# Two attention stages of a decoder kernel: scores and exponents handled by single PSUM bank, the norm a step earlier, the tops' read-back later

## The reference, cut to what matters

```python
x = _layernorm(x + _L0_attn_ref(x, ...))      # norm, q k v, rope, causal softmax, Wo, then a gelu FFN
x = _layernorm(x + _L0_xattn_ref(x, ctx, ...))
x = _layernorm(x + _L0_ffn_ref(x, ...))       # norm, attention over all positions, then a mixture of experts
# inside an attention, per head h:
scores = q[h] @ k[h].T / sqrt(8)              # + causal mask in the first
att[h] = softmax(scores) @ v[h]
```

## Time and profile before

| | |
|---|---|
| median of 3 runs | 2877.28 us (2876.09 to 2885.17) |
| the profiled execution | 2881.1 us, span of the trace 2879.3 us |
| mean granted TensorE clock | 0.860 |
| busy over the span | PE 2162.3 us (75%), PEld 1334.6 (46%), DVE 1974.9 (69%), ACT 1383.5 (48%), POOL 1329.9 (46%) |
| stage `at0`, 56 to 300 us | PE 210.8 of 244 us |
| stage `at1`, 774 to 990 us | PE 148.5 of 216 us |

### The profile page before, as it was taken

One profiled execution on the slowest core, in us unless ns is written; L12 is line 12 of the kernel. 1 busy time (PEld: TensorE's weight loads), 2 busy tenths in 40 slices (PEclk: granted clock), 3 DMA queues, 4 the chain that ended last, 5 costly groups with the idle time before them and its releaser, 6 DMA issues. The chain is left out here.

```text
span 2879.3 us, 48880 instructions
## 1 busy us (share of the span) xinstructions
PE 2162.3 (75%) x19339; PEld 1334.6 (46%) x19339; DVE 1974.9 (69%) x3225; ACT 1383.5 (48%) x2007; POOL 1329.9 (46%) x1015
## 2 busy tenths in 40 slices
PE   3889666776367699999689999999899975553703
PEld 1455444555145566666345554554445543342303
DVE  4565455887455456666358988888988884887576
ACT  1444315554155533333176666666666642221497
POOL 3432244555333100000059889898898892332001
PEclk7899877787578899999789999999999997665856
DMA  4331010000243110000122222222222221000001
GB/s 104 78 89 47 10 32 18 18 16 5 69 99 82 37 55 1 1 1 1 43 67 78 78 76 78 72 85 80 69 78 75 75 67 33 15 15 9 0 0 30
DMA packets 137521, 135.76 MB, mean 47 GB/s; under 512 B 22720, under 2 KB 131024, under 8 KB 134096
## 3 DMA queue, kind: packets, MB, share of 16 engines
q1 hardware_dynamic: 129744, 131.07, 15.8%
q10 hardware_dynamic: 7552, 1.58, 0.3%
HBM read 109.73 MB, written 16.58 MB: 44 GB/s over the span
## 5 line engine op out<-in xcount | busy, mean ns | idle before, releaser
L2293 POOL TENSOR_TENSOR mam_h<-mam_h,mam_c_all 128x1024 f32<-128x1024 f32 x256 | 658.0, 2585 | 91.2 <-DVE mam_h L2365 91.2
L2365 DVE TENSOR_TENSOR_SCAN mam_h<-mam_decay,mam_ps_b 128x1024 f32<-128x1024 f32 x256 | 574.9, 2275 | 101.0 <-PE mam_ps_b L1996 95.3
L1996 PEld LDWEIGHTS mam_ps_b<-mam_diag,mam_duT 64*128 64x128 f32 x4096 | 255.1, 193 | 217.4 <-DVE mam_h L2365 127.0
L2187 ACT ACTIVATE mam_decay<-mam_delta,mam_a_neg 128x508 f32<-128x508 f32 x512 | 331.4, 710 | 32.8 <-DVE mam_h L2365 28.6
L1996 PE MATMUL mam_ps_b<-mam_diag,mam_duT 64*128 64x128 f32 x4096 | 301.1, 290 | 53.8 <-DVE mam_h L2365 42.0
L760 DVE TENSOR_REDUCE at_top<-at_ps_s 128x8 f32<-128x1024 f32 x128 | 156.8, 1225 | 197.8 <-PE at_ps_s L485 196.5
L2015 PE MATMUL mam_ps_y<-mam_h,all_ident 64*64 64x512 f32 x2048 | 255.1, 614 | 13.6 <-POOL mam_h L2293 13.6
L1513 ACT ACTIVATE moe_silu<-moe_ps_g 128x512 f32<-128x512 f32 x144 | 85.9, 597 | 227.3 <-PE moe_ps_g L1456 205.2
L624 ACT ACTIVATE at_e<-at_ps_e 128x1024 f32<-128x1024 f32 x128 | 131.2, 1025 | 116.4 <-PE at_ps_e L485 112.2
L2269 POOL TENSOR_TENSOR mam_diag<-mam_halves,mam_b_col 128x512 f32<-128x512 f32 x128 | 137.6, 1075 | 41.3 <-ACT mam_b_col L2161 41.3
L1468 PEld LDWEIGHTS moe_ps_d<-moe_w_down,moe_hidden 128*128 128x128 f32 x1152 | 139.8, 192 | 33.9 <-issue 33.9
(11 more groups left out here) (357 smaller groups left out, 4503.3 us busy)
## 6 DMA issues: line engine op xcount, KB each, us to landing
mam_c_all<-mam_c_rows SPq DMA_DIRECT2D x256, 256.0 KB, 3.4
at_rows<-at_split SPq DMA_DIRECT2D x64, 192.0 KB, 2.9
at_q<-at_rows SPq DMA_DIRECT2D x32, 192.0 KB
at_k<-at_rows SPq DMA_DIRECT2D x32, 192.0 KB
at_q<-at_rows SPq DMA_DIRECT2D x32, 128.0 KB
at_k<-at_rows SPq DMA_DIRECT2D x32, 128.0 KB
all_x_all<-in_x SPq DMA_DIRECT2D x8, 256.0 KB, 4.8
at_q<-at_rows SPq DMA_DIRECT2D x32, 64.0 KB
```

The lines of the kernel that those rows point to most:

```text
L1996: last = nc.tensor.matmul(ps_b[:, slot, odd, :, at // 2, x:x + HT], duT[r, d, s % DT, at, :], diag[r, chunk % SLOTS, at, :, :], start=True ...
L2187: last = nc.scalar.activation(decay[:, s % SLOTS, :, n, :, 1:T], src, ACT.Exp, scale=a_neg[:, d, s % DT, st:st + 1])
L2293: nc.gpsimd.tensor_tensor(flat(h[:, slot, :, :, :, :]), flat(h[:, slot, :, :, :, :]), flat(c_all[:, chunk, :, :, :, :]), ALU.mult).then_in ...
L2365: nc.vector.tensor_tensor_scan(row(h[:, s % H_SLOTS, :, :, :, :]), row(decay[:, s % SLOTS, :, :, :, :]), row(ps_b[:, s % 2, :, :, :, :]), ...
```

## The change

`both` works one bank at a time: in its first pass the scores' bank 0 (upper rows) with the exponents' bank 1 (lower rows), in its second the scores' bank 1 with the exponents' bank 0. Waits and masks are per bank too. `find_top` becomes two reductions and `exponentiate` two activations, each waiting for its bank and each counted, so the counts that others wait for double. The norm's statistics and root move from step 3 to step 2, and the application from the end of step 0 to the end of the step 3 before it. `read_top(s-2)` moves to the end of ACT's step, behind the second `exponentiate`.

```diff
--- before.py
+++ after.py
@@ -459,56 +459,57 @@
                     return last
                 fill(("v", n), emit)
 
-            def scores_free(b, x):
+            def scores_free(b, x, r):
                 slot, cols = slot_of(b)
-                if x == 0 and b % G == 0:
+                if x == 0 and r == 0 and b % G == 0:
                     for which in range(2):
                         pe.wait_ge(landed[which][slot], LANDED * (b // G // RING + 1))
                 if b > 0 or x > 0:
-                    pe.wait_ge(top_ready, 2 * b + x)
-
-            def exponents_free(b, x):
-                if x == 0:
+                    pe.wait_ge(top_ready, 4 * b + 2 * x + r - 1)
+
+            def exponents_free(b, x, r):
+                if x == 0 and r == 1:
                     pe.wait_ge(top_landed[b % 2], 16 * 2 * (b // 2 + 1))
                 if b > 0 or x > 0:
-                    pe.wait_ge(e_ready, 2 * b + x)
-
-            def masks(b, x, dst, stationary, moving):
+                    pe.wait_ge(e_ready, 4 * b + 2 * x - r)
+
+            def mask(dst, r, stationary, moving):
+                nc.tensor.matmul(dst[:, r, :, :], stationary[:], repeat(moving[:], NJ), start=True, stop=False, skip_group_check=True)
+
+            def product(b, x, r, j, dst, left, right, rows):
+                slot, cols = slot_of(b)
+                at = slice(r * HALF, r * HALF + rows)
+                return nc.tensor.matmul(dst[:, r, j, :], left[at, slot, NJ * x + j, cols], right[at, slot, NJ * x + j, cols],
+                                        start=(not rope and j == 0), stop=(j == NJ - 1), skip_group_check=True)
+
+            def both(s, x):
+
+                now, then = batch(s), batch(s - LAG_E)
                 for r in range(2):
-                    nc.tensor.matmul(dst[:, r, :, :], stationary[:], repeat(moving[:], NJ), start=True, stop=False, skip_group_check=True)
-
-            def products(b, x, dst, left, right, rows, done):
-                slot, cols = slot_of(b)
-                for j in range(NJ):
-                    for r in range(2):
-                        at = slice(r * HALF, r * HALF + rows)
-                        last = nc.tensor.matmul(dst[:, r, j, :], left[at, slot, NJ * x + j, cols], right[at, slot, NJ * x + j, cols],
-                                                start=(not rope and j == 0), stop=(j == NJ - 1), skip_group_check=True)
-                        if j == NJ - 1:
-                            last.then_inc(done, 1)
-
-            def both(s, x):
-
-                now, then = batch(s), batch(s - LAG_E)
-                if now:
-                    scores_free(s, x)
-                    if rope:
-                        masks(s, x, ps_s, c.ident_b, c.causal_b)
-                if then:
-                    exponents_free(s - LAG_E, x)
-                    if rope:
-                        masks(s - LAG_E, x, ps_e, c.causal_b, c.ident_b)
-                if now:
-                    products(s, x, ps_s, q64, k64, SLOTS * HD, s_ready)
-                if then:
-                    products(s - LAG_E, x, ps_e, k64, q64, SLOTS * HD + NS, e_filled)
+                    if now:
+                        scores_free(s, x, r)
+                        if rope:
+                            mask(ps_s, r, c.ident_b, c.causal_b)
+                    if then:
+                        exponents_free(s - LAG_E, x, 1 - r)
+                        if rope:
+                            mask(ps_e, 1 - r, c.causal_b, c.ident_b)
+                    for j in range(NJ):
+                        if now:
+                            scored = product(s, x, r, j, ps_s, q64, k64, SLOTS * HD)
+                            if j == NJ - 1:
+                                scored.then_inc(s_ready, 1)
+                        if then:
+                            filled_e = product(s - LAG_E, x, 1 - r, j, ps_e, k64, q64, SLOTS * HD + NS)
+                            if j == NJ - 1:
+                                filled_e.then_inc(e_filled, 1)
 
             def values(b):
                 slot = b // G % 2
                 if b % G == 0:
                     bank, at = AT[("v", b // G)]
                     pe.wait_ge(taken[bank], at + 1)
-                pe.wait_ge(e_ready, 2 * b + 2)
+                pe.wait_ge(e_ready, 4 * b + 4)
                 if b > 0:
                     pe.wait_ge(attU_ready, b)
                 for k in range(NK):
@@ -618,11 +619,12 @@
                 nc.scalar.copy(split[:, which, 1, :], rest[:, which, :]).then_inc(second_ready[which], 1)
 
             def exponentiate(b, x):
-                act.wait_ge(e_filled, (2 * b + x + 1) * 2)
                 if x == 0 and b >= 2:
                     act.wait_ge(pv_ready, b - 1)
-                nc.scalar.activation(e[:, b % 2, 2 * x:2 * x + 2, :, :].rearrange("p k j t -> p (k j t)"), ps_e[:].rearrange("p r j t -> p (r j t)"),
-                                     ACT.Exp, scale=HD ** -0.5).then_inc(e_ready, 1)
+                for n, r in enumerate((1, 0)):
+                    act.wait_ge(e_filled, 4 * b + 2 * x + n + 1)
+                    nc.scalar.activation(e[:, b % 2, 2 * x + r, :, :].rearrange("p j t -> p (j t)"), ps_e[:, r, :, :].rearrange("p j t -> p (j t)"),
+                                         ACT.Exp, scale=HD ** -0.5).then_inc(e_ready, 1)
 
             def copy_u(b):
                 act.wait_ge(pv_ready, b + 1)
@@ -664,8 +666,6 @@
                     split_first(n + LEAD, r - 2)
                 if batch(s - LAG_E):
                     exponentiate(s - LAG_E, 0)
-                if batch(s - 2):
-                    read_top(s - 2)
                 if r == 1 and come and not rope:
                     copy_compact("q", n + LEAD, 0)
                 if r == 2 and go:
@@ -680,6 +680,8 @@
                     write_top(s - 1)
                 if batch(s - LAG_E):
                     exponentiate(s - LAG_E, 1)
+                if batch(s - 2):
+                    read_top(s - 2)
 
         @block.gpsimd
         def _(pool):
@@ -703,7 +705,7 @@
                 nc.gpsimd.tensor_tensor(split[:, which, 2, :], rest[:, which, :], split[:, which, 1, :], ALU.subtract).then_inc(third_ready[which], 1)
 
             def split_top(b):
-                pool.wait_ge(top_ready, 2 * b + 2)
+                pool.wait_ge(top_ready, 4 * b + 4)
                 if b >= 2:
                     bank, at = AT[("t", b - 2)]
                     pool.wait_ge(filled[bank], at + 1)
@@ -727,7 +729,7 @@
                     split_third(n + LEAD, r - 2)
                 if batch(s):
                     split_top(s)
-                if r == 3 and whole(n + LEAD + 1):
+                if r == 2 and whole(n + LEAD + 1):
                     before.root(nc, pool, c, n + LEAD + 1)
                 if rope and r == 3 and whole(n - LAG_O):
                     g = n - LAG_O
@@ -754,10 +756,11 @@
                     before.apply(nc, dve, x, lambda b: xn[:, b, :], n, xn_ready)
 
             def find_top(b, x):
-                dve.wait_ge(s_ready, (2 * b + x + 1) * 2)
                 if x == 0 and b >= 2:
                     dve.wait_ge(split_ready, b - 1)
-                nc.vector.tensor_reduce(top[:, b % 2, :, NJ * x:NJ * x + NJ], ps_s[:], AX_X, ALU.max).then_inc(top_ready, 1)
+                for r in range(2):
+                    dve.wait_ge(s_ready, 4 * b + 2 * x + r + 1)
+                    nc.vector.tensor_reduce(top[:, b % 2, r, NJ * x:NJ * x + NJ], ps_s[:, r, :, :], AX_X, ALU.max).then_inc(top_ready, 1)
 
             def turn_half(name, n, which, part):
                 if n > 0 and part == 0:
@@ -822,12 +825,12 @@
                     copy_v(n - 1)
                 if batch(s - LAG_U):
                     divide(s - LAG_U)
-                if r == 3 and whole(n + LEAD + 1):
+                if r == 2 and whole(n + LEAD + 1):
                     norm(n + LEAD + 1, 0)
                 if r == 3 and 0 < n + LEAD + 1 < RING:
                     nc.vector.memset(k64[:, n + LEAD + 1, :, :], 1.0).then_inc(ones_ready, 1)
-                if r == 0 and n + LEAD > 0 and whole(n + LEAD):
-                    norm(n + LEAD, 1)
+                if r == 3 and whole(n + LEAD + 1):
+                    norm(n + LEAD + 1, 1)
             bank, at = AT[("o", NG - 1)]
             dve.wait_ge(taken[bank], at + 1)
 
```

## The result

The changed kernel takes 2863.2 us (median of 6, 2861.1 to 2869.6), the kernel before 2878.3 beside it: a ratio of 0.9946, 95% interval 0.993 to 0.9961. So it is faster by 15 us, which is 0.5%. I had forecast 48 us and a range of 2798 to 2866: the median lies just inside the range's upper end, but the gain is a third of what I said.

The account below looks back on a forecast made before the run. PE was taken as nearest to a bound, with 101 us of idle time to win. Terms summed to -15 us in the first attention and -35 in the second, 2 given back: -48, so 2830 us, range 2798 to 2866.

Parts of the forecast that it names:

- 33.7 us: PE's waits for the exponentials in the second attention, taken to be mostly ACT's read_top waiting for the write to land.
- so 24.0 us go: Normalised input ready a step before PE transposes it: waits of 13.3 us (first attention) and 10.7 (second) vanish.
- 2 us for reappearing stalls: Allowance in the sum over both attentions: 2 us given back for stalls that come back elsewhere.
- Banks: Single-bank maxima gain 19.3 us, exponentials 2; after costs in PE's order this part was put at 7.6.
- rival 5: Scores and exponents products stop running side by side: 59 us more on 128 half steps, 2888 us; chance 3%.
- Mode switches: First attention's masks switch PE's array twice more per half step, 0.09 us each: 10 us taken, bounds 0 and 28.
- cost (b): First and last four steps run one product kind, unpaired: 0.23 us more per half step, 3.7 us taken, bounds 0 and 7.4.
- Late read-back: read_top after the second exponential nearly ends waits of 34.7 us in the second attention; 16 return, gain 18.7.
- Reads in steps 0 and 1 will land in 5 to 7 us, like the writes: Landing time assumed for the moved read_top, costing up to 1.9 us twice a group at the following write_top.
- 16 us for what remains of ACT's waits: Second attention: write_top still waits for the read to land, 2 us per group, 16 us; 0 in the first.
- Rival 4: Slower, about 2917 us, chance 5%: write_top in steps 1 and 2 waits for the previous step's read; loses from 7.8 us landings.
- rival 2: Waits only change places: array switches cost 28 us, 24 of ACT's 34.7 return at write_top; 2860 us, chance 21%.

Follow-up runs that it names:

- spread reads: Each repeated row read of k issued as single DMAs of 8 rows, same bytes: 2849.6 us on the kernel before, 2814.7 us on the changed kernel.
- experiment 4: The kernel before with the norm's move alone: 2871.8 us, ratio 0.9967.
- experiment 1: The changed kernel with read_top back at its old place behind the first exponential, norm and banks still changed: 2866.4 us, ratio 0.9947.
- experiment 12: The kernel before with read_top moved behind the second exponential and nothing else changed: 2874.5 us, ratio 0.998.

## Why the prediction was wrong, point by point

*What bounds the kernel.* PE's idle time was the right thing to count, and its releasers were read rightly. I read the 33.7 us as a wait that belongs to the place of `read_top`. It depends on SP's row reads at least as much: the same place with the spread reads leaves 19.1, and the new place with the old reads 43.3. What one wait freed, the next gave back. In the old kernel the form of the k reads is worth 31 us (2849.6), of which 9.4 are at the heads of the two stages.

*Norm.* PE's waits for it went as said, 24 us; the kernel gained 9 (experiment 4), and 14 with the spread reads. The step that failed is "so 24.0 us go". I gave back 2 us for reappearing stalls in both attentions; it was 15 for this part alone. Its profile has 8.9 and 16.5 us more of waits behind the exponentials and 7.3 more behind the first k rows, which is more than the 24. The gain of 9 us that remained stands in PE's own work: for the same instructions PE is busy 228.7 us instead of 235.6 up to the first mark, at a mean granted clock of 0.90 instead of 0.87, and 162.2 instead of 168.0 in the second attention, where the clock is no higher (0.77 and 0.78) and the reason isn't shown. The prediction had no such term.

*Banks.* The prices and the waits for the maximum came as forecast, the pairs held (eight products of the two kinds start between 198.61 and 198.79), rival 5 is out. The part by itself gave about 9, forecast 7.6.

*Mode switches.* 0.21 us for two in the half step shown and 0.19 by PE's busy time (12.3 us in 64), forecast 0.18. The rule of the Trainium skill (TensorEngine Tiling (Array Packing), Key Properties) that changing the tiling mode drains TensorE, which I had named against this part, agrees with the rows in kind. The 0.09 read from the old trace was nearly the price; taking it out again is worth 8 us at the end of the first attention. The cost (b) did not appear: eight products of one kind in a row take 0.41 us (the last row below), where they took 0.40 before (at 986.39). But where PE has to wait for the second bank, four take 0.39 us by themselves, and no term stood for that:

```profile
784.79 0.39 PE L482 MATMUL at_ps_s<-at_k,at_q 48*128 48x128 bf16 x4 [0.43 <-DVE at_top L763]
785.39 0.40 PE L482 MATMUL at_ps_s<-at_k,at_q 48*128 48x128 bf16 x4 [0.20 <-DVE at_top L763]
...
980.52 0.41 PE L482 MATMUL at_ps_e<-at_q,at_k 51*128 51x128 bf16 x8
```

From norm alone to norm and banks PE's busy time grows by 17.4 us in the first attention and 7.7 in the second; the switches are 12.3 of it.

*Late read-back.* This is the term that failed most: a gain of 18.7 us was forecast, and the place gave nothing beside the two other parts (experiment 1) and 6 us alone (experiment 12). The step is "Reads in steps 0 and 1 will land in 5 to 7 us, like the writes". It was taken from the write's landing; the read takes 11.9 us in the row shown. The write of the earlier trace rows had been issued 12.9 us behind the first row read of its group, this read 3.3 us behind it. But the write of the earlier trace rows, 2.1 us behind it, landed in 6.1, so the place in the burst alone doesn't explain the difference, and what else does is open. The read's own landing time stood in no row, because next to nothing waited for it.

I took 16 us for what remains of ACT's waits as PE feels them in the second attention and 1.8 in the first; it was 43.3 and 14.9, and 4.9 for the read itself. That is 27 + 13 + 5 = 45 us more. The two waits for the first k rows, which I had left out, add 6.7. At the mark behind the second attention 41 of the 48 us are missing; set against the 52 are 2.4 us of waiting for the read that was there before, 3.4 less behind POOL's `split_top`, 2.2 less of PE's own work (11.0 and 0.5 us more, forecast 13.7), and the 2 that I had given back. Rival 4's mechanism, then, with its place as described, but rival 2's size: from 7.8 us on I had it slower than before. With a landing of 12 us the formula's 32 waits would have cost 200 us. Only 15 came (66.5 us on ACT), one a group and not two; as I read it, an ACT that stands makes the following step late and the next wait short.

*The rivals.* Rival 2 (21%) gave 2860, and the kernel measured 2863; its reason was right in one half (write_top) and wrong in the other (switches at 0.22 each), so its near hit is in part luck. So is it that the median lies inside my own range.

What isn't settled: why 8 engines carry the row reads at 87 to 95 GB/s where about 3 carry 68, why the read-back takes twice as long as the write of the earlier trace rows, and why the norm's move lengthens the wait for the first k rows.

## What to carry to other kernels

When a wait ends by a DMA, price the DMA by what else is queued then. Here a small transfer beside a burst landed late in it (at 186.9, with the burst over at about 192), and time won elsewhere was then handed over at that wait. The view of the read-back gave no landing time while nearly nobody waited for it; before such a transfer is moved to where someone waits, bound it by the length of the burst beside it and not by the landing of its neighbour. Look at the head of a stage too: its one wait for the first data can grow unseen outside the steady rounds. And single out the parts: here three gave 9, 9 and 6 us alone and 15 together, and 35 together once the row reads were spread.

## What the runs showed of the hardware that was not expected

Repeated DMAs (source step 0 over 3 or 2) kept 4.2 falling to 1.8 of 16 DMA engines busy at 81 to 42 GB/s, and the same bytes as single DMAs 9.4 to 8.0 at 95 to 87 GB/s. 12 KB beside them landed in 11.9 and 10.3 us, where the median write of the maxima lands in 1.5 us in the kernel before and 2.4 in the changed one.

And DVE's application of the norm met POOL in its new place. The four of a group with POOL's addition to y beside them, in the changed kernel, and the four of a group before:

```profile
202.35 2.08 DVE L170 TENSOR_SCALAR at_xn<-all_x_all,at_before_moments,at_before_rstd 128x128 f32<-128x128 f32 x4 [0.17 <-DVE at_att L796]
202.47 1.35 POOL L739 TENSOR_TENSOR all_y_all<-all_y_all,at_b_o 128x512 f32<-128x512 f32 x1
```

```profile
214.14 1.12 DVE L170 TENSOR_SCALAR at_xn<-all_x_all,at_before_moments,at_before_rstd 128x128 f32<-128x128 f32 x4
```

2.08 us instead of 1.12, and PE waits 0.88 us for the maximum behind them (at 205.08). One of the four takes 1.30 us, where the median is 0.34. Two more groups beside this addition took 2.13 and 2.14 us (at 141.1 and 170.3), and one beside POOL's small `split_top` instructions alone 1.18 (at 113.1). That POOL's instruction is the cause was not tried apart.
